# Own units spread two by two, an eleventh ring entry, and the first ring loads held behind the first node tiles

## What is computed

```
# layer 0: a blend of adj and the identity, rows divided by their sums, then a linear map
A' = alpha*adj + (1-alpha)*I
h  = relu((A' @ x) / A'.sum(1) @ W.T + b)
x1 = layernorm(x + h)
# layer 1: attention on adj and on its transpose
xt = logmap0(x1)
par = adj   * sigmoid(xt@w_par[:d][:,None] + xt@w_par[d:][None,:] + b_par)
chi = adj.T * sigmoid(xt@w_chi[:d][:,None] + xt@w_chi[d:][None,:] + b_chi)
out = layernorm(x1 + proj(expmap0((chi + par) @ xt)))
```

## Time and profile before

| | |
|---|---|
| median of three runs | 2229.6 us (2229.26 to 2233.3) |
| profiled execution, its own time | 2234.23 us |
| its span, first to last instruction | 2232.4 us |
| busy: PE, DVE, POOL, ACT | 2035.9, 1938.1, 1334.0, 1324.6 us |
| matrix and other loads on SP's queue | 792.77 MB |
| mean granted TensorE clock | 0.978 |

### The profile page before, as it was taken

How to read it: one execution, slowest core, us unless ns; L and a number is a source line. 1 busy time by engine, 2 the same in 40 slices (tenths; PEclk the granted TensorE clock), 3 DMA queues, 4 the chain that set the end, 5 groups by cost and what they waited for, 6 DMA issues and landing times.

```text
span 2232.4 us, 18671 instructions
## 1 busy us (share of the span) xinstructions
PE 2035.9 (91%) x5248; PEld 921.2 (41%) x5248; DVE 1938.1 (87%) x1856; ACT 1324.6 (59%) x1508; POOL 1334.0 (60%) x607
## 2 busy tenths in 40 slices
PE   6999999999999999998999977998888888889896
PEld 3444444444434444444444433343344334334433
DVE  5757778988989988898998889998998988989996
ACT  0001324354364454453444578988889989999996
POOL 0000305435455455643633577999998998999996
PEclk9999999999999999999999978999999999999998
DMA  9978988999889988888988998999999999998984
GB/s 342 358 274 297 391 301 359 379 357 373 362 341 405 396 346 356 345 357 324 385 337 340 396 421 318 422 375 420 421 408 385 421 420 381 421 421 342 421 352 190
DMA packets 129222, 818.28 MB, mean 367 GB/s; under 512 B 14928, under 2 KB 27472, under 8 KB 33376
## 3 DMA queue, kind: packets, MB, share of 16 engines
q1 hardware_dynamic: 113104, 792.77, 88.2%
q10 hardware_dynamic: 16016, 24.32, 3.2%
HBM read 808.59 MB, written 8.45 MB: 366 GB/s over the span
## 4 chain that ended last, share of the span: by engine, by line
PE 44%; POOL 17%; issue 11%; DVE 11%; ACT 10%; DMA 5%; ACTq 1%; DVEq 0%; POOLq 0%; SPq 0%
PE ps L1129 28%; POOL chi L541 13%; PE ps L1201 11%; DVE dsum L904 3%; ACT chi L724 3%; DMA ring<-in_g_blk 3%; DVE ps L1002 3%; POOL xA L541 3%; ACT ps L741 2%; DMA ring<-in_a_cols 2%; PE ps L1217 1%; DVE keys L1011 1%; POOL acc L550 1%; ACT L724 1%; ACT xA L724 1%
## 5 line engine op out<-in xcount | busy, mean ns | idle before, releaser
L541 POOL TENSOR_TENSOR chi<-chi,ring 128x1024 f32<-128x1024 f32 x321 | 822.1, 2577 | 668.6 <-ACT chi L724 609.8
L1201 PE MATMUL ps<-keys,xtA 128*128 128x512 f32 x2048 | 978.1, 610 | 130.4 <-DVE keys L1011 96.8
L1129 PE MATMUL ps<-ring,xA 128*128 128x512 f32 x2048 | 922.3, 600 | 45.3 <-DMA ring<-in_g_blk 24.9
L741 ACT ACTIVATE ps<-scores,prcr 128x1024 f32<-128x1024 f32 x472 | 521.8, 1106 | 397.4 <-DVE keys L1011 381.2
L1201 PEld LDWEIGHTS ps<-keys,xtA 128*128 128x128 f32 x2048 | 377.9, 193 | 657.3 <-issue 621.4
L904 DVE TENSOR_TENSOR dsum<-dsum,ring 128x2048 f32<-128x2048 f32 x240 | 592.1, 2467 | 23.6 <-DMA ring<-in_g_blk 16.9
L1129 PEld LDWEIGHTS ps<-ring,xA 128*128 128x128 f32 x2048 | 389.3, 192 | 537.6 <-issue 500.5
L1011 DVE TENSOR_TENSOR keys<-ps,chi 128x1024 f32<-128x1024 f32 x426 | 521.6, 1224 | 81.7 <-issue 28.4
L1002 DVE TENSOR_TENSOR ps<-ps,ring 128x1024 f32<-128x1024 f32 x378 | 462.1, 1223 | 76.1 <-ACT ps L741 72.7
L724 ACT ACTIVATE chi<-scores,prcr 128x1024 f32<-128x1024 f32 x426 | 483.8, 1136 | 16.1 <-DMA scores<-plcl_d 8.9
L541 POOL TENSOR_TENSOR chi<-chi,xA 128x1024 f32<-128x1024 f32 x105 | 247.3, 2376 | 26.2 <-ACT chi L724 26.2
(11 more groups left out here) (111 smaller groups left out, 829.4 us busy)
## 6 DMA issues: line engine op xcount, KB each, us to landing
ring<-in_g_blk SPq DMA_DIRECT2D x460, 1024.0 KB, 9.3
ring<-in_a_cols SPq DMA_DIRECT2D x187, 1024.0 KB, 9.9
xA<-in_a_cols SPq DMA_DIRECT2D x69, 1024.0 KB, 11.1
xA<-in_g_blk SPq DMA_DIRECT2D x32, 1024.0 KB, 12.6
scores<-plcl_d ACTq DMA_DIRECT2D x22, 512.0 KB, 8.1
xA<-in_x_g ACTq DMA_DIRECT2D x64, 64.0 KB, 10.2
yb<-in_xT ACTq DMA_DIRECT2D x8, 512.0 KB, 8.9
x_d<-res ACTq DMA_DIRECT2D x8, 512.0 KB, 9.0
```

The costliest lines, as they stand in the source:

```text
L541: pool.tensor_tensor(out=chi(n), in0=chi(n), in1=half(t, n), op=ALU.mult).then_inc(m2_ready, 1)
L741: act.activation(dst, scores[:, row, 0, :], ACT.Sigmoid, bias=prcr[:, 2 * jt:2 * jt + 1]).then_inc(p_ready, 1)
L1129: ins = pe.matmul(Y[:, h * BANK:(h + 1) * BANK], xA[:, tile * D:(tile + 1) * D], t[:, tt * BP + h * BANK:tt * BP + (h + 1) * BANK], start= ...
L1201: ins = pe.matmul(outp[:, h * BANK:(h + 1) * BANK], xtA[:, jt * D:(jt + 1) * D], keys(n)[:, h * BANK:(h + 1) * BANK], start=begins, stop=i ...
```

## The change

There are five edits.

1. The own units of a panel no longer stand in one run: two own units alternate with two others, from position 32 of the group on for panel 3 and position 20 for the other panels, so that a block of 8 own units covers 14 units.
2. The four natural blocks of the own units are loaded together ahead of the block, and their entries are held until the last turn. In the late stage the next load takes the entry that a small function (`given_back`) foresees to be free first, instead of the oldest.
3. The score rows of the late groups use two buffers instead of three. The third becomes an eleventh ring entry, from the load of unit 182's natural block on.
4. A unit is direct only if no own unit lies two ahead of it or two behind: 28 direct units instead of 37.
5. At the start SP issues two ring loads and waits for the first group of node tiles (`x_in0`) before the third, and for the second group (`x_in1`) before the fifth.

```diff
+OWN_BEHIND_FIRST, OWN_BEHIND = 32, 20
...
-            tiles = rest + list(own) if p < NPAN - 1 else rest[:24] + list(own) + rest[24:]
+            at = OWN_BEHIND_FIRST if p == EARLY else OWN_BEHIND
+            tiles = rest[:at]
+            for i in range(0, TPP, 2):
+                tiles += [own[i], own[i + 1], rest[at + i], rest[at + i + 1]]
+            tiles += rest[at + TPP:]
...
-        kinds += [("nat", c)] if 2 * c in OWN_AT else [("nat", c), ("trn", c)]
+        if 2 * c not in OWN_AT:
+            kinds += [("nat", c), ("trn", c)]
+        elif OWN_AT[2 * c] % TPP == 0:
+            kinds += [("nat", OWN[OWN_AT[2 * c] + k] // 2) for k in range(0, TPP, 2)]
...
+    def given_back(e):
+        kind, j = held.get(e, ("pair", 0))
+        if kind == "pair":
+            return -1
+        return OWN[OWN_AT[2 * j] // TPP * TPP + TPP - 1] - 2 if 2 * j in OWN_AT else 2 * j + 1
...
-        e = entries.pop(0)
+        if kind == "nat" and 2 * j == (ENDS[ROWS_GONE] + 16) // 2 * 2:
+            entries.insert(0, RING + EXTRA)
+        e = min(entries, key=given_back) if i >= late + RING - 1 else entries[0]
+        entries.remove(e)
...
-            b = buf % 3
+            b = buf % 2
...
-APART = {n for n in range(MORE + 8, UNITS) if n % 8 == 2 and n not in OWN_AT}
+APART = {n for n in range(MORE + 8, UNITS) if n % 8 == 2 and not {n - 2, n, n + 2} & set(OWN_AT)}
...
+            if e == RING + EXTRA:
+                return scores[:, 2, :, :].rearrange("p k c -> p (k c)")
...
+                if kind == "pair" and j in (2, 4):
+                    sp.wait_ge(x_in[j // 2 - 1], 64)
```

More of the change, by code:

```diff
@@ L175 @@
 SLOT_OF_UNIT, SLOT_OF_NORMS, SLOT_OF_FINAL = slot_plan()
+ROWS_GONE = max(k for k, (p, _, a) in enumerate(GROUPS) if p == 2 and a < NPAN - 1)
 def load_plan():
@@ L348, in natural_of_own @@
         def natural_of_own(n, k):
-            return loaded("nat", (OWN[OWN_AT[n] // TPP * TPP] + k) // 2), k % 2
+            return loaded("nat", OWN[OWN_AT[n] // TPP * TPP + k] // 2), k % 2
         def loaded(kind, j):
@@ L377, in adj_resnorm_kernel @@
         x_in = [sem(f"x_in{G}") for G in range(NG)]
-        r_in = [sem(f"r_in{e}") for e in range(RING + EXTRA)]
+        r_in = [sem(f"r_in{e}") for e in range(RING + EXTRA + 1)]
         l_in = [sem(f"l_in{k}") for k in range(3)]
@@ L461, in wait_free @@
                 if before is None:
-                    if e >= RING:
+                    if e == RING + EXTRA:
+                        sp.wait_ge(c_ready, ENDS[ROWS_GONE] + 1)
+                        sp.wait_ge(p_ready, ENDS[ROWS_GONE] + 1)
+                    elif e >= RING:
                         sp.wait_ge(l0_used, PAIRS)
```

## The result

The changed kernel takes 2252.3 us (median of 4 runs, 2249.4 to 2256.5) against 2231.45 us (4 runs) for the kernel before: ratio 1.0097, 95% interval 1.0082 to 1.0113. It is slower by 21 us, where the forecast had it faster by 5.6. Two further timings gave 2251.3 and 2249.0 us. (One of the executions behind the first of these took 2280.4 us, at a mean granted clock of 0.929 where the other five had 0.970 to 0.975; it widens that interval.)

A forecast was written before the change was run, and what follows sets the result against it. The prediction took POOL, idle only for ACT and never for transfers, to bound the late stage, with PE near full in layer 0. Terms -1.6, -6.8, +2.8 and 0 gave -5.6 us: 2224.0 from 2229.6, range 2216 to 2230.5.

The forecast's parts named there:

- the ring's: Ring entries held around own blocks: queue nearly never idles, data come no later; 0, or +2.5 us without its cover.
- the ring falls short: Own blocks: longer-held entries idle the queue, PE waits, 3 us lost in each of five blocks, 2239 us; chance 0.10.
- its first sign: Own blocks: PE waits for the fourth own block before the first turn, over 2.7 us.
- its arithmetic of 188 us a period: Late stage: transfers need 179 us plus 9 us idle a period, 188 against 185.3.
- The eleventh entry speaks against it: Late ring: the added entry was the argument against transfers falling behind in own blocks, a case given 0.10.
- Nine direct units less, +2.8: Late stage: nine more adds on DVE cost 2.8 us, between 0 and 11.0.
- three times 0.6: Norms of panels 0, 1 and 2 come late for POOL inside the blocks, +1.8 us together.
- DVE's lag is forgotten at every stall of POOL: Late stage: POOL's stalls give DVE time, so the extra adds' cost lies nearer 0 than 11.0 us.
- Own units apart, -6.8: Ends of panels 3 to 6: ACT's copies stop waiting for PE, -5.8, and come sooner, -1.0; between 0 and -8.
- The start, -1.6: Layer 0's start: node tiles come sooner; of 7.5 us about 1 to 4 survives the fourth group, -1.6.
- The sum: Whole kernel: start -1.6, own units -6.8, direct units +2.8, ring 0, together -5.6 us.
- The rule of the Trainium skill: Start: an engine drains some 9 to 17 descriptors per queue turn, so node tiles hardly wait; -7.5 instead of -1.6 us.

The follow-up runs named there:

- the halved loads: Half of each late transposed block not loaded: the kernel before took 2228.55 us, the changed kernel without its start edit 2231.5 us.
- held_14: Kernel before with two row buffers, eleventh ring entry and entries taken as freed, own units in one piece, own entries held six units longer: 2236.9 us.
- fewer_direct: Kernel before with nine direct units taken out, nothing else: 2235.95 us, ratio 1.0023.
- half_trn_apart_36: Changed kernel without its start edit, half of each late transposed block not loaded, blocks of panels 4 to 7 behind 36 others instead of 20: 2231.9 us.
- rows_alone: Kernel before with only two row buffers, the third as eleventh ring entry, and entries taken as they come free: 2229.4 us, ratio 0.9990.
- half_trn_before: Kernel before with only half of each late transposed block loaded: 2228.55 us, ratio 0.9993.
- piece_48: Changed kernel without its start edit, own units of panels 3 to 6 in one piece behind 48 others, panel 7 at 24: 2230.7 us, ratio 1.0001.
- start_alone: Kernel before with only the start's ring loads held back for the first two groups of node tiles: 2230.6 us, ratio 0.9999.

## Why the prediction was wrong

**The step that failed** is the ring's: "It nearly never idles, and data come no later than now", priced at 0 with a bound of +2.5. It cost 12.0 us (the halved loads); a hold of this length by itself, at the old place of the piece, cost 7.5 (`held_14`). What the clock's falls in the blocks cost is inside the 12.0 and was not parted from it. The error was in how I read rows 5. I took the queue's 6.2 us of idle time in an own run for slack, since POOL didn't wait, and compared the ring with one block only: up to 7 loads unlanded at its start. But the period's balance decides, and it was nearly closed: 5 to 7.5 us to spare in 185. With 11.0 us of idle time the lead was used up by the second block, and the 7 unlanded loads became nine, so that a load issued at 1551 lands at 1572. The 29 us for the hold were too short as well: from the first turn of panel 4's block, at 1564.75, to the end of its last, at 1604.95, 40.2 us pass, since POOL's stops for the late load and behind the root lie inside it, and the block of panel 3, which has neither, took 32.6. The first block (units 200 to 213) shows it: it starts with data landed 14 us ahead and costs nothing; that of panel 4 starts with 1 us.

The rival "the ring falls short" had this mechanism, its first sign (PE waiting before the first turn) and its arithmetic of 188 us a period (192.1 measured). I gave it 0.10 and 3 us in each of five blocks; in fact three periods paid, some 6 to 7 us each (192.1, 191.0 and 189.9 against 185.3, 185.2 and 183.4), the waits behind the roots included. "The eleventh entry speaks against it" weighed too much, though without it and its order the loss would have been 75 us. The row with PE's 3.4 us of waits for own blocks in the kernel before should have raised the chance.

**Nine direct units less, +2.8.** Right in kind, too small: 5.3 us in `fewer_direct`. The term "three times 0.6" for the norms measured 2.1 each (4.39 against 2.29 us). The statement that DVE's lag is forgotten at every stall of POOL holds only where there is a stall before the next one that needs DVE; `half_trn_apart_36` showed that the lag, moved away from one such place, is paid at another.

**Own units apart, -6.8.** The waits of ACT's copies went, 5.8 us to 0, as said, but less came of it. From the first to the ninth unit at the four ends (units 232, 304, 376, 448 and eight on) POOL took 100.5 us before and 97.1 after. In `rows_alone`, where nothing is mixed, it is 97.7 already, and in `half_trn_before`, which has none of the edits, 97.6. So most of those 3.4 us came from transfers that were late at the own turns before, and edit 3 is enough to mend them. With halved loads the mixing makes 93.7 out of 97.6. This term was thus some -3.9 us where the data came in time and near nothing where they came late. `piece_48`, without a wait at the copies and without a gain, says the same: the wait at a group's end is in part a debt of PE and DVE, which is paid elsewhere.

**The start, -1.6.** Nothing measurable in the time. `x_in1` came without a stop, as said; `x_in2` was put at 27.4 us and came at 32.1. The 0.5 us that were left there (32.14 against 32.68) turned into 1.4 us of loss by the 65th product (47.87 against 46.49 us), through the clock that fell while PE stood. The term reckoned every product at its full speed.

**The sum** by measured terms (without edit 5 it comes out by construction, being made of the same differences): ring +12.0, order and direct units +2.95, edit 5 between 0 and 6 beside the mixed units; 15 without edit 5 (measured 14.7 and 15.3), 15 to 21 with it (measured 18.5 to 21). The direct units' +5.3 and the four ends' -3.9 are both inside the 2.95; the experiments don't part them exactly, since the nine units of `fewer_direct` aren't the changed kernel's.

The rule of the Trainium skill (DMA: Bandwidth & Descriptors, section Queues, rings and completion order) would have let the node tiles pass and given -7.5 us at the start. No run shows that gain: `start_alone` is at 0.9999. But this isn't a clean test of the rule. From 8 to 21 us the changed kernel's ACT queue moved 2291 packets, against 665 before, 1213 of them under 512 bytes: the constants, which stand ahead of `x_in2`. And what came of the start was taken back in part by the clock.

## What to carry to other kernels

Where the transfers of a period take nearly the whole period, idle time of the queue isn't slack but the last of it: add the bytes at full rate and the idle time over several whole periods before anything holds ring entries longer, and look at the lead between landing and use, which a chain of waits doesn't show until it is gone. Here three more held units cost nothing and six cost 7.5 us. When an engine with little idle time gets more work, look for every later instruction that needs it early: moving one of them only moves the bill. And look at the granted clock wherever a change makes PE start earlier and stop later: here the later start with the shorter stops was as fast.

## What the runs showed of the hardware

With the queue full, loads of 1 MB landed 2.5 us apart whatever the entry, and the time from issue to landing grew with their number, to some 21 us with eight or nine under way. Halving the rows of every second load of the late stage (from 8 KB to 4 KB) let the rate over a period fall from 406 to 316 GB/s and made the kernel before only 2.1 us faster.

In all five traces in which PE stood 4 to 7 us for `x_in2`, the granted clock fell to half the full one in that stop or at its end, for 3.4 to 10.2 us. In the block of panel 4 it fell in the second of two stops of 2 us, for some 7 us, and four products took 3.62 us there instead of 1.88.
